# Attention layer with 8 heads: head pairs in 32-row tiles of TensorE, one pipeline over all PSUM banks

## What is computed

```python
xn = groupnorm(x)                         # 32 groups of 2 channels
gfeat = mean(xn) @ gproj_w.T + gproj_b    # one value per channel
q, k, v = split(conv1x1(xn, qkv_w) + qkv_b)   # 8 heads of 8 channels
k = k + 0.1 * gfeat
attn = softmax(q.T @ k * 8 ** -0.5)       # per image and head, 256 x 256
out = proj_w @ (attn @ v) + proj_b + 0.1 * gfeat + x
```

## Time and profile before

| | us |
|---|---|
| median of 3 runs | 101.08 (101.0 to 101.27) |
| profiled execution, first to last instruction | 100.9 |
| PE busy | 87.6 |
| DVE busy | 66.3 |
| ACT busy | 47.3 |
| POOL busy | 22.5 |

### The profile page before, as it was taken

The page is one execution under the profiler, slowest core; times in us unless marked ns, Lnnn a source line. Parts: engine busy times, 40 slices in busy tenths (PEclk is TensorE's granted clock), DMA queues, the critical chain, the costliest instruction groups (busy, mean ns, idle before and its releaser), DMA issues.

```text
span 100.9 us, 1683 instructions
## 1 busy us (share of the span) xinstructions
PE 87.6 (87%) x577; PEld 65.2 (65%) x577; DVE 66.3 (66%) x178; ACT 47.3 (47%) x111; POOL 22.5 (22%) x46
## 2 busy tenths in 40 slices
PE   5996977699899999766994999999999899999660
PEld 5874735478679687464893899766776675566220
DVE  1247699978674997598566627788968875543401
ACT  3329366445595525300232242727665848766310
POOL 7963000000000020212075276087043000000000
PEclk9999999999999999996559655999999999999975
DMA  2940000000000000000000000000000000000101
GB/s 69 307 186 0 0 0 0 6 0 0 0 3 3 0 0 0 0 0 6 0 0 0 0 0 0 0 0 6 0 0 0 0 6 0 0 3 0 52 6 52
DMA packets 1304, 1.79 MB, mean 18 GB/s; under 512 B 144, under 2 KB 912, under 8 KB 1296
## 3 DMA queue, kind: packets, MB, share of 16 engines
q1 hardware_dynamic: 1008, 1.48, 4.5%
q10 hardware_dynamic: 288, 0.20, 0.7%
HBM read 1.42 MB, written 0.26 MB: 17 GB/s over the span
## 4 chain that ended last, share of the span: by engine, by line
PE 66%; DVE 20%; ACT 9%; issue 3%; DVEq 0%
PE PS L446 11%; PE PS L479 9%; PE PS L466 7%; PE PS L432 6%; PE PS L294 6%; PE PS L341 6%; ACT E L709 6%; DVE KM L983 3%; PE PS L456 3%; DVE NM L989 3%; PE PS L353 3%; DVE NM L878 3%; PE PS L490 2%; DVE E L894 2%; PE PS L304 2%
## 5 line engine op out<-in xcount | busy, mean ns | idle before, releaser
L989 DVE TENSOR_REDUCE NM<-PS 128x2 f32<-128x512 f32 x32 | 21.9, 690 | 7.0 <-PE PS L446 6.8
L742 ACT ACTIVATE E<-PS 128x1024 f32<-128x1024 f32 x16 | 16.3, 1024 | 11.6 <-PE PS L466 11.6
L269 POOL TENSOR_TENSOR KM<-QKS,W 128x512 fp32r<-128x512 f32 x14 | 14.3, 1041 | 21.0 <-ACT QKS L733 21.0
L446 PE MATMUL PS<-KM,QKS 128*128 128x256 f32 x64 | 15.6, 335 | 3.8 <-DVE KM L983 2.5
L709 ACT ACTIVATE E<-PS,NM 128x256 f32<-128x256 f32 x24 | 11.1, 473 | 11.9 <-DVE NM L878 11.8
L446 PEld LDWEIGHTS PS<-KM,QKS 128*128 128x128 f32 x64 | 11.1, 218 | 7.4 <-DVE NM L989 3.6
L294 PE MATMUL PS<-idle 128*128 128x256 f32 x65 | 13.7, 350 | 1.2 <-DVE idle L838 1.2
L294 PEld LDWEIGHTS PS<-idle 128*128 128x128 f32 x65 | 11.0, 233 | 3.1 <-DVE idle L838 1.2
L466 PE MATMUL PS<-QSA,KM 128*128 128x256 f32 x64 | 11.5, 305 | 0.0
L466 PEld LDWEIGHTS PS<-QSA,KM 128*128 128x128 f32 x64 | 9.5, 207 | 0.8 <-issue 0.8
L479 PE MATMUL PS<-E,VA 128*32 128x256 f32 x128 | 9.8, 390 | 0.0
(11 more groups left out here) (104 smaller groups left out, 131.0 us busy)
## 6 DMA issues: line engine op xcount, KB each, us to landing
W<-pack SPq DMA_DIRECT2D x1, 384.0 KB, 5.4
W<-pack SPq DMA_DIRECT2D x1, 290.0 KB, 4.9
X<-x SPq DMA_DIRECT2D x2, 128.0 KB, 2.6
W<-pack SPq DMA_DIRECT2D x1, 256.0 KB, 4.5
out<-Y SPq DMA_DIRECT2D x2, 128.0 KB, 1.7
W<-pack ACTq DMA_DIRECT2D x1, 128.0 KB, 3.0
W<-pack ACTq DMA_DIRECT2D x1, 72.0 KB, 2.5
```

Source lines behind the costliest of these rows:

```text
L269: pool.tensor_tensor(KM[p][s % 3][:, heads, :], QKS[p][s % 3][:, 1:2, :].bitcast(f32).broadcast_to([P, 2, N]), w("heads")[:, heads].unsque ...
L446: mm = pe.matmul(bank_a[p][:, half * N:(half + 1) * N], QKS[p][s % 3][:, 0, half * HALF:(half + 1) * HALF], KM[p][s % 3][:, j, :], start=T ...
L742: act.activation(E3[p][s % 2][m][:, :, :].rearrange("k j q -> k (j q)"), bank_bc[p][:, :], ACT.Exp, scale=float(HD) ** -0.5)\
L989: dve.tensor_reduce(NM3[p][:, s % 2, :, j], bank_a[p].rearrange("q (h k) -> q h k", h=2), AX.X, ALU.max, negate=True).then_inc(maxima3[p], 1)
```

## The change

Layers 0 to 2 keep their instructions and their order. In layer 3:

- There is one pipeline of eight units u = 0 to 7 (pair u // 4, image u // 2 % 2, heads u % 2) in place of two interleaved streams. Its banks are those of both pairs: scores of the first two heads in `s_low` (banks a and b of pair 0), those of the other two in `s_high` (banks c and d of pair 1; unit 0 uses s_low for both), transposed scores in `t_banks` (banks a and b of pair 1), the mix in bank c of pair 0, stacks, maxima rows and projection in bank d of pair 0, the turned output in bank a of pair 0 after its last use for scores.
- No masked keys. `score3(u, two)` multiplies 24 rows of one head's queries with the same 24 rows of its keys, and `score_t(u, two)` all 32 rows; both do two heads j, in neighbouring 32-row tiles, with outputs in different banks. The matmul count for scores stays at 64 and 64.
- `maxima_of` covers two heads, 1024 columns, in one instruction (16 in place of 32). `stack_copy` is one 512-column instruction (8 in place of 16). `exps_t` still covers 1024 columns, now two heads and both halves of the keys. The two parts of the maxima are made on POOL (`parts_of_maxima`), two small instructions for each unit. `add_max_rows` now also takes one off the two rows of maxima, because the ones are added to queries and keys alike.
- `o_copy`, `turn3` and `divide3` take two units at a time where they can.
- The `keep_clock` calls within layer 3 shrink from 6 + 4 + 3 + 4 + 1 matmuls to 6.

```diff
-        QKS = [[sb(f"QKS{p}{i}", [P, 2, N], f32r) for i in range(3)] for p in R]
-        KM = [[sb(f"KM{p}{i}", [P, HPG, N], f32r) for i in range(3)] for p in R]
+        QKS = [sb(f"QKS{i}", [P, 2, N], f32r) for i in range(4)]
+        s_low, s_high = PS[0][:, 0:1024], PS[1][:, 1024:2048]
+        t_banks, mix_bank, turn_bank = PS[1][:, 0:1024], bank_c[0], bank_a[0]
+        stack_bank = bank_d[0]
...
+            def parts_of_maxima(u):
+                rows, maxima_u = rows_of_maxima(u), NM3[u % 2][:, :, :]
+                pool.wait_ge(maxima3, 2 * u + 2)
+                if u >= 2:
+                    pool.wait_ge(aug_made, u - 1)
+                pool.tensor_copy(rows[:, :, :, MAXROW], maxima_u).then_inc(max_high, 1)
+                pool.wait_ge(max_high, u + 1)
+                pool.tensor_tensor(rows[:, :, :, MAXROW + 1], maxima_u,
+                                   rows[:, :, :, MAXROW].bitcast(f32), ALU.subtract)\
+                    .then_inc(max_parts, 1)
...
+            def stack(u):
+                if u == 0:
+                    pe.wait_ge(prep_pool, PREPARED)
+                elif u < 3:
+                    pe.wait_ge(stack_out, u)
+                else:
+                    pe.wait_ge(aug_out, u - 2)
...
+            def score3(u, two):
+                pe.wait_ge(stack_out, u + 1)
+                if u == 1 and two == 1:
+                    pe.wait_ge(v_out[1], 4)
+                    pe.wait_ge(stat[1], 10)
+                elif u == 0 and two == 1 or u == 1:
+                    pe.wait_ge(maxima3, u + 1)
+                elif u > 1:
+                    pe.wait_ge(maxima3, 2 * u - 1 + two)
+                if two == 0 and u in (6, 7):
+                    pe.wait_ge(on_out, 1)
+                bank = score_banks(u, two)
+                for half in range(2):
+                    for j in (2 * two, 2 * two + 1):
+                        rows = slice(j * QUAD, j * QUAD + MAXROW)
+                        at = (j % 2) * 2 * N + half * N
+                        mm = pe.matmul(bank[:, at:at + N],
+                                       QKS[u % 4][rows, 0, half * HALF:(half + 1) * HALF],
+                                       QKS[u % 4][rows, 1, :], start=True, stop=True)
+                mm.then_inc(scores3, 1)
+
+            def max_rows(u):
+                pe.wait_ge(max_parts, u + 1)
+                if u + 2 < UNITS:
+                    pe.wait_ge(stack_out, u + 3)
+                else:
+                    pe.wait_ge(aug_out, u)
...
+            def score_t(u, two):
+                pe.wait_ge(aug_out, u + 1)
+                if u == 0 and two == 0:
+                    pe.wait_ge(k_low[1], 1)
+                    pe.wait_ge(q_low[1], 1)
+                else:
+                    pe.wait_ge(exps3, 2 * u + two)
+                for m in range(2):
+                    for j in (2 * two, 2 * two + 1):
+                        rows = slice(j * QUAD, (j + 1) * QUAD)
+                        at = (j % 2) * 2 * N + m * N
+                        mm = pe.matmul(t_banks[:, at:at + N],
+                                       QKS[u % 4][rows, 1, m * HALF:(m + 1) * HALF],
+                                       QSA[u % 2][rows, :], start=True, stop=True)
+                mm.then_inc(scores_t, 1)
...
+            exps_t(3, 0)
+            stack_copy(6)
+            o_copy(0, (0, 1))
+            exps_t(3, 1)
...
-            first_head_keys(0)
             residual(2, 1)
             statistics(1)
-            maxima_of(0, 0, 0)
             values3(0)
+            maxima_of(0, 0)
             group_variance(1)
-            maxima_of(0, 1, 0)
             normalise(1)
             global_feature(1)
-            maxima_of(0, 2, 0)
+            maxima_of(0, 1)
             low_keys(1)
             low_queries(1)
-            maxima_of(0, 3, 0)
+            maxima_of(1, 0)
             values3(1)
-            first_head_keys(1)
+            add_max_rows(0)
+
+            maxima_of(1, 1)
+            maxima_of(2, 0)
+            add_max_rows(1)
```

More of the change, by code:

```diff
@@ L485, in turn3 @@
[L485 to L498 removed]
+                    mm = pe.matmul(stack_bank[:, half * HALF:(half + 1) * HALF],
+                                   AUGW[u % 2][:, half, :], ident_r[:, :], start=True, stop=True)
@@ new lines, in mix3 @@
+            def mix3(u):
+                p, b, g = u // 4, u // 2 % 2, u % 2
+                pe.wait_ge(exps3, 2 * u + 2)
+                pe.wait_ge(v_out[p], 4)
+                if g == 0 and u > 0:
+                    pe.wait_ge(o_out, u // 2)
+                for m in range(2):
+                    for j in range(HPG):
+                        mm = pe.matmul(mix_bank[j * QUAD:(j + 1) * QUAD, g * N:(g + 1) * N],
+                                       VA[p][:, m, b, g * HPG + j, :], E3[u % 2][:, j, m, :],
+                                       start=(m == 0), stop=(m == 1))
+                mm.then_inc(mixed3, 1)
@@ new lines, in turn3 @@
+            def turn3(batch, groups, n):
+                pe.wait_ge(o_out, n)
+                if n > 1:
+                    pe.wait_ge(on_out, n - 1)
+                if batch < 2:
+                    pe.wait_ge(maxima3, 4 * batch + 11)
+                for g in groups:
+                    for half in range(2):
+                        at = (2 * g + half) * P
+                        tp = pe.transpose(turn_bank[:, at:at + P],
+                                          OS[batch % 2][:, g, half * HALF:(half + 1) * HALF], ident)
+                tp.then_inc(turned3, 1)
@@ L654, in _ @@
-            turn3(2, 0)
-            score_t(3, 0, 1)
-            turn3(0, 1)
-            turn3(3, 0)
-            mix3(2, 0, 1)
-            mix3(2, 1, 1)
+            score3(1, 0)
+            max_rows(0)
+            score3(1, 1)
+            score_t(0, 0)
+            score3(2, 0)
+            stack(3)
+            score_t(0, 1)
+            score3(2, 1)
+            max_rows(1)
+            score_t(1, 0)
+            score3(3, 0)
+            stack(4)
+            score_t(1, 1)
+            score3(3, 1)
@@ new lines, in _ @@
+            max_rows(2)
+            mix3(0)
+            score_t(2, 0)
+            score3(4, 0)
+            stack(5)
+            score_t(2, 1)
+            score3(4, 1)
+            max_rows(3)
+            mix3(1)
+            score_t(3, 0)
+            score3(5, 0)
+            stack(6)
+            score_t(3, 1)
+            score3(5, 1)
+            max_rows(4)
+            mix3(2)
+            turn3(0, (0, 1), 1)
+            score_t(4, 0)
+            score3(6, 0)
+            stack(7)
@@ L660, in _ @@
+            score_t(4, 1)
+            score3(6, 1)
+            max_rows(5)
+            mix3(3)
+            score_t(5, 0)
+            score3(7, 0)
+            score_t(5, 1)
+            score3(7, 1)
+            max_rows(6)
+            mix3(4)
+            turn3(1, (0, 1), 2)
+            score_t(6, 0)
+            mix3(5)
+            score_t(6, 1)
+            max_rows(7)
+            score_t(7, 0)
             back3(0)
-            turn3(1, 1)
-            score_t(3, 1, 1)
+            mix3(6)
@@ L663, in _ @@
+            score_t(7, 1)
+            turn3(2, (0, 1), 3)
             out3(0)
-            turn3(2, 1)
-            mix3(3, 0, 1)
-            mix3(3, 1, 1)
-            turn3(3, 1)
+            turn3(3, (0,), 4)
+            mix3(7)
+            turn3(3, (1,), 5)
             back3(1)
@@ new lines, in _ @@
+            maxima_of(3, 1)
+            maxima_of(4, 0)
+            add_max_rows(3)
+            maxima_of(4, 1)
+            maxima_of(5, 0)
+            add_max_rows(4)
+            divide3(0, (0, 1), 1)
+            maxima_of(5, 1)
+            maxima_of(6, 0)
+            add_max_rows(5)
+            maxima_of(6, 1)
+            maxima_of(7, 0)
+            add_max_rows(6)
+            divide3(1, (0, 1), 2)
+            maxima_of(7, 1)
+            add_max_rows(7)
+            divide3(2, (0, 1), 3)
@@ L1228, in packed @@
                                    np.isin(rows[:C] // HID1 % KINDS1, K_LOW)]))
-    column("ones_rows", (rows % QUAD == MAXROW) | (rows % QUAD == MAXROW + 1))
-    put("heads", rows[:, None] // QUAD == np.arange(HPG))
+    ones = (rows % QUAD == MAXROW) | (rows % QUAD == MAXROW + 1)
+    column("ones_rows", ones)
+    column("minus_ones_rows", -1.0 * ones)
     put("ident", np.eye(P))
```

554 lines of the change are left out of this document (155 added, 399 removed).

## The result

The changed kernel is slower: 109.2 us median of four executions (107.7 to 110.0), the kernel before 101.2 beside it; the ratio is 1.072, 95% interval 1.061 to 1.082. The forecast was 95.8 us with a range to 100.2. The profiled execution has a span of 107.8 us at a time of 109.98.

What follows compares the result with a forecast made beforehand. PE bounds the middle of layer 3, waits before it, and a three-engine chain ends it. First exponential 5.9 us earlier, 1.4 saved in the pipeline, 2.0 given back to the clock: 101.08 - 5.3 = 95.8 us, range 92.5 to 100.2.

Steps and rivals of the forecast that it cites:

- What bounds the way to the first exponential, and when it comes: Start of layer 3: without masked keys the first exponential starts about 54.2 us (53.5 to 56), 5.9 us earlier.
- One unit: Layer 3 pipeline: period 3.75 us, set by stack copy, max_rows and mix3 on PE, paired score matmuls running together.
- Rival C: Layer 3 score matmul pairs run in series, 0.22 us more a call, 3.5 us in all, 99.3 us; chance 0.07.
- The clock: PE in layer 3: full clock from about 57 us, 0.50 from about 80 us on, giving back 2.0 us.
- Rival B: Low clock never or only briefly leaves layer 3, since row tiles use a quarter of the array: 104.5 us; chance 0.08.
- The price of a unit at the low clock: Layer 3 pipeline: 3.2 us of PE work x 1.7 = 5.5 us a unit at the low clock.
- The factor 1.7: PE work at the low clock costs about 1.7 times as much (stack: 1.15 against 0.67 us).
- The pipeline's own gain: Layer 3 pipeline of eight units: 1.4 us saved at full clock, beyond the earlier start.
- Unit 4 with its division: Layer 3: DVE divides first (0.75 us), delaying maxima, POOL, max_rows and mix3; the unit takes 4.5 us.
- The comparison of times: Whole kernel: span before 100.9 us set against median 101.08, 0.2 us between; forecast span 95.6 became 95.8 us.

Runs made afterwards that it cites:

- the run with the clock held: Changed kernel plus 128-row matmuls of zeros where TensorE waits, before and in the pipeline: 99.5 and 99.7 us at clock 0.99 to 1.00, otherwise 102.1 to 112.2.

## Why the prediction was wrong

**What bounds the way to the first exponential, and when it comes: right.** 54.56 us against 54.2, with the steps close to those worked out: residual at 43.01 (forecast 42.6), low parts' end at 51.1 (51), wide maxima 1.22 us (1.24), first score_t at 53.73 (53.4).

**One unit: right in its size at the full clock.** 3.91 against 3.75 us (the run with the clock held), with zeros in it that the forecast did not have, the stack copy 0.69 (0.7), POOL's pair 0.20 and 0.21 us. The pairs do run together: two in 0.58 us, four in 0.80 at the low clock, where a single one takes 0.58:

```profile
60.74 0.58 PE L440 MATMUL PS<-QSA,QKS 32*128 32x256 f32 x2
...
60.74 0.80 PE L440 MATMUL PS<-QSA,QKS 32*128 32x256 f32 x4
```

Rival C (in series) is out: in series a unit is 7.64 instead of 5.93 us. The Trainium skill (TensorE: Matmul & The Clock Gate, Part 3) has tiles in different row groups start about 4 ns apart. These rows agree: both matmuls of the first pair start at 60.74 us and end within 0.58, the time of one.

**The clock: the step that failed.** The forecast let it return at about 57 us and fall at 80, for 2.0 us. It stayed low from 47 to 77.6 and, with three breaks of 3.4 us, to the end. By pieces, up to the end of the result: 0.4 us at the first exponential; from there to the first exponential of unit 7 39.0 us instead of 28.3, 10.7 us; from there to the result's end at 105.6 12.1 instead of 11.1, 1.0 us. With the clock held the second piece was 32.1 us (54.02 to 86.12) with one low stretch in it, where a unit took 5.81 instead of 3.91. So I estimate 8.8 of the 10.7 us as the low clock, and 1.9 as units that are longer than forecast at the full clock. Rival B was this case, at 104.5 us and 0.08. What I set against it was wrong in two ways: "at the low clock PE becomes full, and full PE came before a clock of 1.00" made a rule of one stretch of 128-row matmuls, and PE busy for 28.4 of 30.6 us did not bring the clock back in the changed kernel; and layer 1's 32-row scores "amid clock 1.00" are eight matmuls in two groups of four. That 128-row scores would have kept it is what the runs with the same columns in 32 and in 128 rows bear out; why the clock comes back after 3 us in one execution and after 30 in another stays open. The price of a unit at the low clock, 5.5 us, was also short by 0.4. The factor 1.7 was right (1.15 against 0.66 for four stack matmuls), but PE's work in a unit was taken as 3.2 us and is 3.5 without the zeros in the rows above, since a score call behind a change of shape takes 0.43 or 0.57 us and not 0.24.

**The pipeline's own gain did not show.** 1.4 us were forecast as saved at a full clock. In the run with the clock held a unit is 3.91 us and more, and the old pipeline has the first exponentials of its stages 3.2 to 4.0 us apart, but for the first two (31.6 us from first to last at the full clock). With the clock held the new one needs 36.3 us (54.02 to 90.35), two low stretches and the zeros in it. Why one pipeline is no shorter than two streams was not tested; that two streams hide each other's waits is my reading of the order. Unit 4 with its division took 0.5 us more than forecast. And from unit 7's first exponential to the last copy of a mix the forecast has 4.85 us; it was 8.0 with the clock held (low from 88.0 to 91.3), and 6.0 with mix3(6) moved (at 1.00 from 87.1 on). The wait of mix3(6) for o_copy(2) was missing in the forecast's path, although moving it changed the times by less than 0.7 us.

**The comparison of times.** I set the span of 100.9 us beside the median of 101.08 and took 0.2 us between them. In the later runs a time is 2.1 to 2.3 us above its own span (1.7 to 1.9 in the two kernels with the first scores in tiles). So I estimate about 103.1 us for the profiled execution of before, with a clock of 0.914; the median belongs to one with 0.96, as executions of 100.6 to 101.3 us have 0.96 in all later runs. The forecast time should have been 2 us higher for the same sum, or the sum's base one with less low clock.

## What to carry to other kernels

Row tiles bought array time here and paid with the clock: before packing small matmuls into tiles, ask whether TensorE will still be granted 2.4 GHz. The busy share of the page did not tell it in this case (93% busy from 47 to 77.6 us at 0.50), and one stretch of the old kernel is no evidence for the new one. Cost such a kernel at both levels, as here a unit of 3.9 us became 5.9, and run it several times, as single executions of one kernel lay between 98.3 and 114.5 us. And before merging two interleaved streams into one pipeline, count the new chain against the old spacing: here 3.9 us against 3.2 to 4.0.

## What the runs showed of the hardware

- TensorE was 99% busy (33.75 of 34 us) at a granted clock of 0.51 with score matmuls of 24 and 32 rows (and three 32-row zeros in each score3), and 86% busy (20.47 of 23.70) at 1.00 with 128 rows. The closest pair is the same columns in the same order: 39.07 of 40 us busy at 0.50 in 32 rows, 20.47 of 23.70 at 1.00 in 128. The Trainium skill (TensorE: Matmul & The Clock Gate, Part 1) has the clock follow how busy the engine has been; by the profile's busy time these rows do not agree.
- Going into another tile shape and out again, with a two-column matmul, cost 0.27 us a call at the full clock (5.30 against 4.24 us a unit of four calls). A group of three zeros ahead of a 32-row call cost 1.23 us at the low clock: 0.64 of columns, 0.30 ahead of them and 0.29 behind.
- A stretch with 17.2 of 23.7 us busy kept 1.00, and one with 30.5 of 30.6 busy stayed at 0.50, most of its scores in 128 rows. Busy shares at the two levels are not the same work, as four stack matmuls take 0.66 us at one and 1.15 at the other.
- The clock record can begin late: in three profiled executions the first change on record is at 24.5 to 24.8 us, the views show 1.00 ahead of it, and 64-row matmuls there take 656 ns instead of about 400. Two of these executions reach the statistics of pair 0 6.6 and 7.1 us later (42.12 against 35.48 us, and 42.21 against 35.13).
- A reduction of 1024 columns over two banks takes 1219 ns, against 690 for 512: 0.16 us less than two.
